# Another order table for the two local-attention layers of a one-core Trainium2 kernel

## The chip, the core and the metric

The kernel runs on one core of one Trainium2 chip. The core has a matmul engine (TensorE, PE in the profile, with its weight loads as PEld), a vector engine (DVE), an activation engine (ScalarE, ACT), a general engine (GpSimd, POOL) and a queue engine that only starts transfers (SyncE, SP). Each engine works through its own list of instructions in order and waits on semaphores where it needs another engine's result. The metric is the device time in microseconds (us), as the median of several executions; lower is better.

## The reference, cut to what matters

Input is `x` of shape (4, 1024, 256) in float32. It is normalised, and the output is `x` plus a gated attention of 16 heads over a window of 64 plus the output of two layers. This is one layer; the change concerns the two layers alone:

```python
def _layer(x, wqkv, qs, ksc, wo, lg, lb, w1, b1, w2, b2):
    h = shift_token(x)                        # half of the columns from the token before
    q, k, v = split(h @ wqkv)                 # 8 heads of 64
    q, k = rotary_xpos(l2norm(q) * qs, l2norm(k) * ksc)
    o = local_attention(q, k, v)              # softmax over a window of 128 keys back
    x = x + o @ wo
    h = layernorm(shift_token(x)) * lg + lb
    a, g = split(h @ w1 + b1)                 # hidden width 682
    return x + (a * gelu(g)) @ w2 + b2
```

## The kernel before, in words

There are two phases. `attention_phase` does the normalisation and the gated attention in the first 650 us; `layers_phase` does the two layers. The layers phase goes over 8 sequences (4 of the batch, for two layers; `it` 0 to 7) and over two halves of 512 tokens each. So the same pass over a half runs 16 times, from 702 us to the end at 1961 us, about 79 us each. I call such a pass a half.

What each engine does in a half is not worked out at run time. The list `ORDER` names 109 steps, and every engine walks the same list and emits its own share of each step. So the place of a step in the list sets where its instructions stand in the list of each engine that has a share of it. Steps that no common engine takes part in may change places freely. Within a half, the attention and feed-forward of this half are done, and at the same time the queries, keys and values of the next half are prepared.

The steps that the prediction speaks of, with what each engine does in them (number n is one of 8 units of two heads and two token tiles, or one of 4 tiles):

- `scores n`: PE, 24 small matmuls (L1497) into one of two pairs of score banks, which waits until `softmax n-2` has read them; DVE, mask and row maximum (L1713, four pieces).
- `softmax n`: ACT, four exponentials (L1639). `weigh n`: DVE, one reciprocal (L1721); POOL, four multiplications (L1380).
- `transpose n`: PE, into two banks (L1508 and L1512); ACT, copies (L1587, L1590, L1591). `values n`: PE (L1530) into `o_bank`; `take_o n` then empties it: ACT (L1645), DVE (L1724).
- `transpose_x`: PE, 8 transposes of the next half's rows (L1423) into two banks; ACT copies the high part (L1599), DVE the low part (L1672).
- `project_qk n`: PE, two products of 12/2 matmuls (L1416); ACT, copy and square of each (L1611, L1617); DVE, sums of squares and a clamp (L1677, L1681); POOL, the power -0.5 (L1362).
- `rope n`: DVE (L1688, L1689), POOL (L1368). `rope_sum n`: DVE (L1696, L1699). `transpose_qk n`: PE (L1469), ACT copies (L1593).
- `up n`: PE, 12 matmuls (L1555), or 6 where n is 5 or 11; ACT gelu (L1655), DVE product (L1775), ACT high part (L1659), DVE low part (L1779). `down n`: PE, 6 matmuls, or 4 where n is 5 or 11 (L1570).
- `load_wqkv`: ACT starts three transfers of 1 MB of weights (L88), once in the run, in the first half of `it` 3, since the layer changes after that sequence. `load_x`: SP starts the load of the rows that a later `transpose_x` reads.

PE writes all transposes and products in turn into three banks; a fill waits until the bank's last content, three fills back, has been taken:

```python
def take_bank(it, n):
    fill = filled.upto(it, n) - 1
    if fill >= 3:
        pe.wait_ge(*vacated(fill - 3))
    return bank_of(it, n)
```

`project_qk` counts as taken when DVE has summed its squares, `transpose` and `transpose_qk` when ACT has copied them, `transpose_x` when DVE has taken the low part.

## Time and profile before

| | us |
|---|---|
| median of 3 runs | 1965.38 |
| lowest and highest run | 1961.76, 1968.51 |
| the profiled execution, its own time | 1963.38 |
| its span, first to last instruction | 1961.3 |
| its mean granted TensorE clock | 0.982 |
| PE busy | 1836.3 (94%) |
| ACT, DVE, POOL busy | 1377.8, 1244.0, 903.6 |
| a half, between the ends of two | 78.6 to 80.3 |

All views below are of this one execution. Times at the start of a row are us from the start of the span. A row of the timeline has start, duration, engine, line, operation with its tiles, and how many instructions it merges; in brackets stands how long the engine was idle before it and who ended that. The half shown most is the one from 938.5 us, the second half of the second sequence.

### The profile page before, as it was taken

What the parts mean: (1) busy time and instruction counts of PE and PEld (TensorE: products, weight loads), DVE (VectorE), ACT (ScalarE), POOL (GpSimd) and SP (SyncE); (2) the same over time, 40 slices, a digit from 0 to 9 for tenths busy, and PEclk for the clock granted to TensorE, in tenths of its full rate; (3) what the DMA queues carried; (4) which work ended last, traced back from release to release, by engine and by line L of the source; (5) the groups of instructions that cost most, each with busy time, mean ns of one, the idle gap of its engine ahead of it and who ended that gap; (6) DMA issues with size and microseconds to landing.
All of it is one profiled execution on the core that took longest, in us unless ns stands there. A gap on an engine that the chain in (4) does not pass through costs nothing.

```text
span 1961.3 us, 47714 instructions
## 1 busy us (share of the span) xinstructions
PE 1836.3 (94%) x17808; PEld 1565.5 (80%) x17808; DVE 1244.0 (63%) x4126; ACT 1377.8 (70%) x3998; POOL 903.6 (46%) x1302
## 2 busy tenths in 40 slices
PE   6999999999999789999999999999999999999998
PEld 4788788788778568788788887887888878888787
DVE  4544543454443467777777777777777776777765
ACT  5886987878688465766857757668577585675854
POOL 3533543434344553735626437255364562654621
PEclk9999999999999889999999999999999999999989
DMA  4321320422324511110110101305112112010110
GB/s 146 100 76 55 116 87 34 116 76 77 87 75 150 180 47 28 39 53 23 47 45 23 54 17 50 122 15 168 37 39 63 34 47 66 18 60 25 42 47 28
DMA packets 125018, 128.11 MB, mean 65 GB/s; under 512 B 26632, under 2 KB 100082, under 8 KB 124788
## 3 DMA queue, kind: packets, MB, share of 16 engines
q1 hardware_dynamic: 121620, 118.77, 19.5%
q10 hardware_dynamic: 3168, 6.29, 0.9%
q8 instruction: 142, 2.33, 0.5%
q14 instruction: 88, 0.72, 0.1%
HBM read 72.44 MB, written 36.85 MB: 56 GB/s over the span
## 4 chain that ended last, share of the span: by engine, by line
PE 58%; ACT 11%; DVE 11%; POOL 11%; issue 5%; DMA 2%; SPq 1%; DVEq 0%; POOLq 0%; ACTq 0%
PE a_bank L630 15%; PE f_bank L1555 10%; PE f_bank L1416 9%; PE f_scores L1570 5%; POOL f_prob L1380 5%; PE a_o_bank L727 4%; ACT f_prob L1639 3%; PE f_o_bank L1530 3%; PE f_scores L1497 3%; PE a_bank L712 2%; PE a_scores L704 2%; POOL f_qk_tok L1368 2%; DVE f_scores L1713 2%; POOL f_norm L1362 1%; POOL a_prob L610 1%
## 5 line engine op out<-in xcount | busy, mean ns | idle before, releaser
L610 POOL TENSOR_SCALAR a_prob<-a_prob,a_row_inv,a_gate 128x128 f32<-128x128 f32 x512 | 226.3, 459 | 379.9 <-DVE a_row_inv L948 379.9
L1380 POOL TENSOR_SCALAR f_prob<-f_prob,f_row_inv 128x192 f32<-128x192 f32 x512 | 244.6, 495 | 319.6 <-DVE f_row_inv L1721 319.6
L1416 PE MATMUL f_bank<-weights,f_actT 128*128 128x512 f32 x1152 | 300.7, 406 | 1.5 <-DVE f_actT L1672 1.5
L1555 PE MATMUL f_bank<-f_hT,f_w 128*128 128x256 f32 x2112 | 269.1, 283 | 1.0 <-DVE f_gu L1775 1.0
L1555 PEld LDWEIGHTS f_bank<-f_hT,f_w 128*128 128x128 f32 x2112 | 258.4, 188 | 4.0 <-DVE f_gu L1775 2.7
L1416 PEld LDWEIGHTS f_bank<-weights,f_actT 128*128 128x128 f32 x1152 | 209.6, 191 | 48.2 <-ACT f_probT L1587 3.1
L1368 POOL TENSOR_TENSOR f_qk_tok<-f_qk_tok,tables 128x512 f32<-128x512 f32 x128 | 164.8, 1308 | 149.3 <-DVE f_sin_part L1689 149.3
L1639 ACT ACTIVATE f_prob<-f_scores,f_neg_max 128x192 f32<-128x192 f32 x512 | 207.9, 426 | 17.2 <-DVE f_neg_max L1713 15.9
L1713 DVE CUSTOM_DVE_ANT_0 f_scores<-f_scores,f_mask 128x192 f32<-128x192 f32 x512 | 166.3, 387 | 69.3 <-PE f_scores L1497 69.2
L1362 POOL TENSOR_TENSOR f_norm<-f_norm,f_minus_half 128x16 f32<-128x16 f32 x64 | 189.3, 2959 | 34.4 <-DVE f_norm L1681 31.5
L630 PE MATMUL a_bank<-a_xT,weights 128*128 128x512 f32 x768 | 195.6, 405 | 1.5 <-DVE a_wgate L917 1.5
L838 ACT ACTIVATE a_prob<-a_scores,a_neg_max 128x128 f32<-128x128 f32 x512 | 179.4, 391 | 24.1 <-DVE a_neg_max L939 24.0
L1659 ACT ACTIVATE f_u<-f_gu 128x256 fp32r<-128x256 f32 x192 | 80.2, 418 | 152.2 <-DVE f_gu L1775 152.2
L630 PEld LDWEIGHTS a_bank<-a_xT,weights 128*128 128x128 f32 x768 | 143.1, 191 | 36.8 <-issue 3.1
L1779 DVE TENSOR_TENSOR f_u<-f_gu,f_u 128x256 fp32r<-128x256 f32 x192 | 98.4, 513 | 93.0 <-ACT f_u L1659 93.0
L1570 PE MATMUL f_scores<-f_w,f_u 128*128 128x256 f32 (+1 forms) x1088 | 150.5, 283 | 0.0
L1497 PE MATMUL f_scores<-f_kT,f_q 64*64 64x128 f32 (+2 forms) x3072 | 117.9, 286 | 32.4 <-ACT f_prob L1639 31.7
L939 DVE CUSTOM_DVE_ANT_0 a_scores<-a_scores,a_mask 128x128 f32<-128x128 f32 x512 | 129.9, 324 | 26.0 <-PE a_scores L704 25.8
L1497 PEld LDWEIGHTS f_scores<-f_kT,f_q 64*64 64x64 f32 x3072 | 98.6, 137 | 56.9 <-ACT f_prob L1639 35.1
L1570 PEld LDWEIGHTS f_scores<-f_w,f_u 128*128 128x128 f32 (+1 forms) x1088 | 138.4, 189 | 2.9 <-DVE f_u L1779 1.5
L1655 ACT ACTIVATE f_gu<-f_bank,f_rows 128x256 f32<-128x256 f32 x192 | 89.6, 467 | 69.2 <-PE f_bank L1555 67.8
L952 DVE TENSOR_TENSOR a_o<-a_o_bank,a_o 128x512 fp32r<-128x512 f32 x64 | 44.1, 689 | 119.8 <-ACT a_o L845 119.8
(143 smaller groups left out, 4021.6 us busy)
## 6 DMA issues: line engine op xcount, KB each, us to landing
split_weights<-a_hi_lo SPq DMA_DIRECT2D x16, 512.0 KB, 3.0
x_next<-states SPq DMA_DIRECT2D x32, 256.0 KB, 3.2
tables<-scaled_tables SPq DMA_DIRECT2D x16, 512.0 KB, 6.0
f_x<-states SPq DMA_DIRECT2D x16, 512.0 KB, 5.3
split_weights<-a_hi_lo SPq DMA_DIRECT2D x12, 682.0 KB, 4.6
weights<-split_weights ACTq DMA_DIRECT2D x6, 1024.0 KB, 9.3
f_w<-split_weights SPq DMA_DIRECT2D x4, 1280.0 KB, 11.7
f_v_crossed<-f_v SPq DMA_DIRECT2D x40, 128.0 KB, 2.4
```

The costliest lines, as they stand in the source:

```text
L610: last = nc.gpsimd.tensor_scalar(part, part, row_inv[:, a % 2, head, t:t + 1], gate[:, half, t, h:h + 1], ALU.mult, ALU.mult)
L630: last = nc.tensor.matmul(out, lhs(c, a), rhs(c, b), start=(i == 0), stop=(i == len(order) - 1))
L838: e = nc.scalar.activation(prob[:, a % 2, head, t, :], scores[a % 2][head][:, t, :], ACT.Exp, bias=neg_max[:, a % 2, head, t:t + 1], scale ...
L1362: nc.gpsimd.tensor_tensor(n, n, minus_half[:], ALU.pow).then_inc(norm_ready.sem, 1)
L1368: last = nc.gpsimd.tensor_tensor(by_head(qk_tok[:, a % TILES])[:, which], by_head(qk_tok[:, a % TILES])[:, which], table(COS, a % TILES)[: ...
L1380: last = nc.gpsimd.tensor_scalar(part, part, row_inv[:, a % 2, head, t:t + 1], 1.0, ALU.mult, ALU.mult)
L1416: last = nc.tensor.matmul(out, lhs(c, a), rhs(c, b), start=(i == 0), stop=(i == len(order) - 1))
L1497: mm = nc.tensor.matmul(scores[a % 2][head][queries, t, place:place + keys.stop - keys.start], q[rows, pair, col:col + P][:, queries], kT[ ...
L1555: mm = nc.tensor.matmul(out[:, which * PART:(which + 1) * PART], w1[:, wp, c, col:col + P], hT[:, hp, c, columns_of(a // FH)], start=(i == ...
L1570: mm = nc.tensor.matmul(y_banks[a // FH % PARTS][:, t, :], u[0:k, a % GATED, up, t * P:(t + 1) * P], w2[0:k, wp, j, :], start=(j == 0 and ...
L1639: last = nc.scalar.activation(prob[:, a % 2, head, t, :], scores[a % 2][head][:, t, 0:KEYS], ACT.Exp, bias=neg_max[:, a % 2, head, t:t + 1 ...
L1713: last = nc.vector.tensor_tensor_reduce(out=sc, in0=sc, in1=mask[:, t + 1 if half or tile or t else 0], scale=-1.0, scalar=3e38, op0=ALU.a ...
```

## The change

Only the table `ORDER` is different: the same steps with the same numbers, in other places. Two of its lines, before and after:

```diff
-ORDER = [("softmax", 0), ("softmax", 1), ("scores", 0), ("scores", 1), ("weigh", 0), ("scores", 2), ("weigh", 1), ("transpose_x", 0),
+ORDER = [("softmax", 0), ("scores", 0), ("scores", 1), ("weigh", 0), ("weigh", 1), ("softmax", 1), ("transpose_x", 0), ("scores", 2),
```

Seen by engine, few places differ in a half. PE: `transpose_x` goes ahead of `scores 2`; `values 2` goes behind `transpose 3` and `project_qk 2`; `down 5` ahead of `up 9`; `transpose_qk 2` ahead of `down 6`; `down 9` ahead of `transpose_qk 3`. ACT: `softmax 3` ahead of `take_o 0`; `take_o 1` ahead of `transpose_qk 0`; `load_wqkv` from behind `transpose_h 1` to the end of the half. DVE: `scores 2` goes behind `weigh 1` and `transpose_x`; `ln_stats 1` goes ahead of `up 2`. POOL: nothing. SP: `load_x` from the first place to behind `shift_back`.

The first place is the start of a half on PE. Before, the 8 transposes of `x_next` (`transpose_x`) stand behind the matmuls of `scores 2` (the last three rows of L1497 ahead of them), and `transpose 0` follows:

```order
L1497 MATMUL f_scores<-f_kT,f_q 64x192 x2
L1497 MATMUL f_scores<-f_kT,f_q 64x128 x2
L1497 MATMUL f_scores<-f_kT,f_q 64x64 x2
L1423 MATMUL f_bank<-ident,x_next 128x128 x8
L1508 MATMUL f_bank<-ident,f_prob 128x128 x4
L1512 MATMUL f_bank<-ident,f_prob 128x128 x2
```

Now the same place reads as follows; the rows of L1497 behind `x_next` are `scores 2`, the one ahead of it is the end of `scores 1`:

```order
L1497 MATMUL f_scores<-f_kT,f_q 64x64 x2
L1423 MATMUL f_bank<-ident,x_next 128x128 x8
L1497 MATMUL f_scores<-f_kT,f_q 64x192 x2
L1497 MATMUL f_scores<-f_kT,f_q 64x128 x2
L1497 MATMUL f_scores<-f_kT,f_q 64x64 x2
L1497 MATMUL f_scores<-f_kT,f_q 64x192 x2
L1497 MATMUL f_scores<-f_kT,f_q 64x128 x2
L1497 MATMUL f_scores<-f_kT,f_q 64x64 x2
L1508 MATMUL f_bank<-ident,f_prob 128x128 x4
```

So the 8 transposes moved from behind a step that waits for `softmax 0` to ahead of it.

The second place is the middle of the attention on PE, around `project_qk 2` (the 12 matmuls of L1416). Before, `values 2` (L1530) comes first, then `transpose 3` (L1508, L1512) and `project_qk 2`:

```order
L1530 MATMUL f_o_bank<-f_probT,f_v 64x256 x2
L1530 MATMUL f_o_bank<-f_probT,f_v 64x64 x2
L1530 MATMUL f_o_bank<-f_probT,f_v_crossed 64x64 x2
L1508 MATMUL f_bank<-ident,f_prob 128x128 x4
L1512 MATMUL f_bank<-ident,f_prob 128x128 x2
L1416 MATMUL f_bank<-weights,f_actT 128x512 x12
```

Now:

```order
L1508 MATMUL f_bank<-ident,f_prob 128x128 x4
L1512 MATMUL f_bank<-ident,f_prob 128x128 x2
L1416 MATMUL f_bank<-weights,f_actT 128x512 x12
L1530 MATMUL f_o_bank<-f_probT,f_v 64x256 x2
L1530 MATMUL f_o_bank<-f_probT,f_v 64x64 x2
L1530 MATMUL f_o_bank<-f_probT,f_v_crossed 64x64 x2
```

`values 2` moved behind both, so PE asks for the banks of `transpose 3` and `project_qk 2` earlier by the length of `values 2`.

The third place is on ACT in the one half in which the weights of the next layer are loaded. Before, the three transfers stand behind the copy of `transpose_h 1` (L1599), amid the gelus:

```order
L1599 ACTIVATE f_hT<-f_bank 128x2x256
L88 DMA weights<-split_weights 128x4x512 x3
L1655 ACTIVATE f_gu<-f_bank,f_rows 128x256
L1659 ACTIVATE f_u<-f_gu 128x256
L1655 ACTIVATE f_gu<-f_bank,f_rows 43x256
```

Now they stand behind the copies of `transpose_qk 3` (L1593), ahead of the next half's first exponentials:

```order
L1593 ACTIVATE f_q<-f_bank 128x4x128
L1593 ACTIVATE f_kT<-f_bank 128x4x128
L88 DMA weights<-split_weights 128x4x512 x3
L1639 ACT_TABLE_LOAD
L1639 ACTIVATE f_prob,f_row_sum<-f_scores,f_neg_max 128x192 x8
```

They moved by seven gelus and to within ten us of their first reader.

## Rows read from the trace of the kernel before

**Rows 1.** The page, busy us (share of the span) of each engine.
```profile
PE 1836.3 (94%) x17808; PEld 1565.5 (80%) x17808; DVE 1244.0 (63%) x4126; ACT 1377.8 (70%) x3998; POOL 903.6 (46%) x1302
```

**Rows 2.** Windows, one half: length, busy us by engine, clock, DMA.
```profile
938.00:1017.00 79.00, 75.56 (x769) 66.54 (x768) 57.88 (x165) 53.92 (x151) 39.26 (x46) 0.98 0.12 36
```

**Rows 3.** Waits of PE from 700 us on: total us, times, longest.
```profile
PE f_scores L1497 <- ACT f_prob L1639: 31.7, 17, 2.1
PE f_bank L1508 <- POOL f_prob L1380: 16.6, 31, 1.2
```

**Rows 4.** Timeline of PE, start of the half.
```profile
938.45 1.75 PE L1497 MATMUL f_scores<-f_kT,f_q 64*64 64x192 f32 x48
942.15 0.89 PE L1497 MATMUL f_scores<-f_kT,f_q 64*64 64x192 f32 x24 [1.95 <-ACT f_prob L1639]
942.97 1.92 PE L1423 MATMUL f_bank<-ident,x_next 128*128 128x128 f32 x8
944.68 1.06 PE L1508 MATMUL f_bank<-ident,f_prob 128*128 128x128 f32 x4
```

**Rows 5.** Timeline of POOL, ACT and DVE in the same stretch.
```profile
942.51 1.62 POOL L1380 TENSOR_SCALAR f_prob<-f_prob,f_row_inv 128x192 f32<-128x192 f32 x4 [16.08 <-DVE f_row_inv L1721]
...
945.55 0.69 DVE L1672 TENSOR_TENSOR f_actT<-f_bank,f_actT 128x512 fp32r<-128x512 f32 x1 [0.16 <-ACT f_actT L1599]
...
945.78 0.60 ACT L1587 ACTIVATE f_probT<-f_bank 128x512 f32<-128x512 f32 x1 [0.26 <-PE f_bank L1508]
...
947.05 0.42 ACT L1639 ACTIVATE f_prob<-f_scores,f_neg_max 128x192 f32<-128x192 f32 x1
```

**Rows 6.** Windows in the same stretch; the clock stands behind POOL's busy time.
```profile
944.00:945.00 1.00, 1.00 (x7) 1.00 (x6) 1.00 (x7) 0.67 (x2) 0.23 (x2) 0.50 0.00 0
```

**Rows 7.** Timeline of POOL through the attention.
```profile
953.20 2.91 POOL L1362 TENSOR_TENSOR f_norm<-f_norm,f_minus_half 128x16 f32<-128x16 f32 x1 [1.63 <-DVE f_norm L1681]
...
966.01 2.91 POOL L1362 TENSOR_TENSOR f_norm<-f_norm,f_minus_half 128x16 f32<-128x16 f32 x1
...
973.01 3.63 POOL L1380 TENSOR_SCALAR f_prob<-f_prob,f_row_inv 128x192 f32<-128x192 f32 x4
...
979.50 1.62 POOL L1380 TENSOR_SCALAR f_prob<-f_prob,f_row_inv 128x192 f32<-128x192 f32 x4
```

**Rows 8.** Timeline of PE at `transpose 7`, and of DVE in `rope_sum 1`.
```profile
978.58 1.03 PE L1469 MATMUL f_bank<-ident,f_qk_tok 128*128 128x128 f32 x8
980.47 0.41 PE L1508 MATMUL f_bank<-ident,f_prob 128*128 128x128 f32 x2 [0.85 <-ACT f_kT L1593]
981.18 0.44 PE L1508 MATMUL f_bank<-ident,f_prob 128*128 128x128 f32 x2 [0.30 <-POOL f_prob L1380]
...
973.75 1.23 DVE L1696 TENSOR_TENSOR f_qk_tok<-f_qk_tok,f_sin_part 128x1024 f32<-128x1024 f32 x1
```

**Rows 9.** Timeline around `project_qk 2`.
```profile
957.79 1.50 DVE L1677 TENSOR_REDUCE f_norm<-f_square 128x8 f32<-128x512 f32 x2
...
958.20 0.77 PE L1530 MATMUL f_o_bank<-f_probT,f_v 128*64 128x256 f32 x8
...
959.25 0.66 PE L1508 MATMUL f_bank<-ident,f_prob 128*128 128x128 f32 x4
...
959.88 3.05 PE L1416 MATMUL f_bank<-weights,f_actT 128*128 128x512 f32 x12
```

**Rows 10.** Timeline of the end of this half.
```profile
1015.53 2.14 PE L1570 MATMUL f_scores<-f_w,f_u 128*128 128x256 f32 x16
...
1016.44 0.42 DVE L1779 TENSOR_TENSOR f_u<-f_gu,f_u 42x256 fp32r<-42x256 f32 x1 [0.48 <-ACT f_u L1659]
```

**Rows 11.** The weight transfers at 1237 us; then PE's first product behind them.
```profile
L88 ACTq DMA_DIRECT2D weights<-split_weights x3: 386/583/596, 1237.2 to 1238.3; - x3
...
DMA to landing us min/median/max: 6.1/8.4/10.5
...
1264.29 3.04 PE L1416 MATMUL f_bank<-weights,f_actT 128*128 128x512 f32 x12
```

More of the change, by code:

```diff
@@ new lines @@
+ORDER = [("softmax", 0), ("scores", 0), ("scores", 1), ("weigh", 0), ("weigh", 1), ("softmax", 1), ("transpose_x", 0), ("scores", 2),
+         ("transpose", 0), ("softmax", 2), ("transpose", 1), ("scores", 3), ("weigh", 2), ("project_qk", 0), ("softmax", 3), ("values", 0),
+         ("take_o", 0), ("load_x1", 0), ("weigh", 3), ("rope", 0), ("values", 1), ("scores", 4), ("transpose", 2), ("project_qk", 1),
+         ("softmax", 4), ("scores", 5), ("transpose", 3), ("weigh", 4), ("rope_sum", 0), ("project_qk", 2), ("values", 2), ("scores", 6),
+         ("softmax", 5), ("weigh", 5), ("rope", 1), ("take_o", 1), ("values", 3), ("transpose_qk", 0), ("transpose", 4), ("scores", 7),
+         ("softmax", 6), ("weigh", 6), ("project_qk", 3), ("project_o", 0), ("transpose", 5), ("softmax", 7), ("values", 4), ("values", 5),
+         ("rope_sum", 1), ("load_tables", 0), ("load_others", 0), ("weigh", 7), ("take_o", 2), ("ln_stats", 0), ("transpose", 6),
+         ("project_v", 0), ("transpose_qk", 1), ("transpose", 7), ("ln_apply", 0), ("take_o", 3), ("rope", 2), ("values", 6), ("values", 7),
+         ("project_v", 2), ("transpose_h", 0), ("project_o", 1), ("rope_sum", 2), ("shift_keys", 0), ("shift_front", 0), ("up", 0),
+         ("up", 1), ("ln_stats", 1), ("up", 2), ("project_v", 1), ("down", 0), ("down", 1), ("project_v", 3), ("ln_apply", 1), ("up", 3),
+         ("down", 2), ("transpose_h", 1), ("rope", 3), ("up", 4), ("down", 3), ("up", 5), ("up", 6), ("up", 7), ("down", 4),
+         ("shift_back", 0), ("up", 8), ("down", 5), ("up", 9), ("rope_sum", 3), ("load_x", 0), ("cross_values", 0), ("transpose_qk", 2),
+         ("down", 6), ("up", 10), ("up", 11), ("down", 7), ("down", 8), ("down", 9), ("transpose_qk", 3), ("add_attended", 0), ("out", 0),
+         ("out", 1), ("load_wqkv", 0), ("down", 10), ("down", 11)]
```

13 lines of the change are left out of this document (removed).

## The prediction

> **What bounds the kernel now.** I read the page first: PE is busy 94% of the span, and ACT, DVE and POOL far less [rows 1]. That share is an average over two phases, and the table is only used in the second, so I asked for windows of one half each. In the half from 938 us PE is busy 75.56 of 79 us [rows 2]. The other 3.4 us are what an order can win; the work itself is the same before and after. Then I read whom PE waits for. Two waits make nearly all of it: `scores 2` waits for the exponentials of `softmax 0`, 31.7 us in 17 waits, so about 2 us in each half; and the transposes of the weighed probabilities wait for POOL, 16.6 us in 31 waits [rows 3].
>
> The timeline shows where these lie. At the start of a half PE issues `scores 0` and `scores 1`, is done at 940.2 us (938.45 + 1.75) and stands idle until 942.15, when ACT has let go of the first score banks [rows 4]. In the stretch that follows, ACT and DVE hand things to each other: the copy of `transpose 0` starts at 945.78 and `softmax 2` at 947.05, behind the copies [rows 5].
>
> The second bound is POOL. It starts the first power of `project_qk 0` at 953.20, after an idle 1.63 us that DVE ended, and from there it has no idle until `weigh 7` ends at 981.12 (979.50 + 1.62) [rows 7]. PE arrives at `transpose 7` at about 979.6 (978.58 + 1.03) and can go on only at 980.47 and 981.18, after the first and the second half of `weigh 7` [rows 8]. The first of these waits is put down to ACT, but POOL's first two pieces end at 980.3 (979.50 + 0.82), so it is POOL. Behind 981.6 PE runs without a gap to the end of the half. So a half is: start (softmax and copies), then POOL's run of 28 us, then PE's 36 us. A gain at the start counts if it moves the start of POOL's run; PE alone has 0.9 to 1.5 us to spare ahead of `transpose 7`.
>
> **The change, part by part.**
>
> Start of the half. `transpose_x` goes into the idle 1.95 us. Its banks are free and its rows are loaded half a pass earlier. Eight transposes take 1.92 us at the low clock [rows 4, 6]; four others take 0.66 at the full one [rows 9], so 8 take between 1.3 and 1.9 us and fit into 940.2 to 942.15. `scores 2` stays where it is, since ACT sets it. `transpose 0` then stands at 943.0 and no longer at 944.68, but its first head comes from POOL at 943.33 (942.51 + 0.82) and its second at 944.13 [rows 4, 5]. I take the end of its first part at 944.55 against 945.74 before. ACT copies the two x banks from 943.6 and 944.1, so ends at 944.7 and not 945.5, and DVE's low parts end 0.6 earlier than 946.24 (945.55 + 0.69). DVE now does `scores 2` only behind them, from 945.6, and its first head is there at 946.4. ACT is through with `transpose 0` at about 946.4 too, so `softmax 2` starts at 946.45 against 947.05 [rows 5]. Gain 0.6 us. From above it is bounded by the whole idle of 1.95 us, from below by 0: if DVE's late `scores 2` takes it back, `softmax 2` stays at 947.0.
>
> Clock. PE idles from 940.2 to 942.15, and the granted clock then falls to 0.50 (1.2 GHz) for about three us, while the x transposes and `transpose 0` run [rows 6]. With 0.8 us of idle ahead of `scores 2` in place of 1.95 the fall may stay away. That helps the 0.6 to come true and I add nothing for it.
>
> POOL's run. `project_qk 0` follows `softmax 2` and the copies of `transpose 1` on ACT, so it moves by the same 0.6, and so does POOL's start. `softmax 3` ahead of `take_o 0` fills an idle moment in which ACT waits for the values; ACT is not what POOL waits for, so I count 0. Inside the run POOL waits at one place nearly for DVE: the power of `project_qk 2` at 966.01 [rows 7].
>
> Middle. `values 2` (1.05 us, from 958.20 to 959.25 [rows 9]) no longer separates `scores 5` from `transpose 3` and `project_qk 2`. `project_qk 2` needs the bank of `project_qk 1`, which DVE frees at 959.29 (957.79 + 1.50) before and 0.4 earlier after, at 958.9. PE would be ready at 958.2, so it waits 0.7 us there, a new stall, and starts at 959.0 in place of 959.88 [rows 9]. `values 2` now follows, so `scores 6` comes at 959.0 + 3.0 + 1.05 = 963.0, against 962.9 before. This eats PE's own gain and leaves it at `transpose 7` as late as before, 979.6; POOL ends there at 980.5 in place of 981.12. Cost 0 as long as PE's slack of 0.9 us covers it. DVE's part of `project_qk 2` even comes earlier, so POOL's power at 966.01 moves along.
>
> A collision on POOL. `weigh 6` takes 3.63 us at 973.01 while `weigh 7` takes 1.62; beside the long one runs DVE's `rope_sum 1` from 973.75 [rows 7, 8]. `rope_sum 1` hangs on PE's `project_o 0`, which I leave where it is, and `weigh 6` starts 0.6 earlier. Then three of its four pieces (0.41 each) are done before DVE starts. That could win up to 2.0 us of POOL's run, of which PE can use 0.9 beyond the 0.6. The other bound is a loss of as much in another place, since `weigh 3` and `weigh 4` would meet other DVE work. I take +0.15 us, near zero, since the two ends are equally far and only the one collision is seen in the row.
>
> The Trainium skill (SBUF — State Buffer, § SBUF: two separate sides) says that POOL and DVE share one port pair as an exclusive lock, also against DVE operations with two SBUF inputs, and that the later one blocks for the whole instruction. `rope_sum` has two SBUF inputs, and 3.63 against 1.62 us agrees. By that rule alone, a `weigh 6` that is ahead would lose nothing and the collision term would be its upper end; the sum would be that of the third rival, 13.5.
>
> End of the half. `down 5` (4 matmuls, at 2.14 / 16 us each [rows 10] 0.5 us) now precedes `up 9`. So the gelu of `up 9`, `rope_sum 3` and the chain of `up 10` and `up 11` on DVE come up to 0.5 later. The last low part ends at 1016.86 (1016.44 + 0.42), and PE needs it for the last four matmuls of the run of 16 that ends at 1017.67, so at 1017.1 [rows 10]: 0.25 us of cover. Loss between 0 and 0.3 us; I take 0.1, since most halves have a DVE that is a little ahead of the one shown. `transpose_qk 2` and `down 9` only change places among PE work, and ACT's copies of `transpose_qk 3` wait for ACT itself: 0. `ln_stats 1` ahead of `up 2` delays that one's low part by 1.4 us, hidden behind the values products on PE: 0. `load_x` is early enough in both: 0.
>
> Once in the run, `load_wqkv` comes right ahead of the half that begins near 1255. Its three issues take ACT about 0.58 us each [rows 11], 1.7 us, and a part of this lies in ACT's wait for the first row maxima (`scores 0` must run and be masked first): I take 0.9. The transfers land 6.1 to 10.5 us after their issue, so at 1261 to 1265 if issued from 1254.5 on, beside the loads of the new half; `project_qk 0` needs the first at 1264.3 and the second 1.5 us later [rows 11]. Loss 0 to 2 more; I take 0.6. Together 1.5.
>
> **Sum**, against the profiled execution of 1963.38 us: 15 halves (the last has no next half to prepare; I leave it at 0) times 0.6 + 0.15 - 0.1 = 0.65 gives 9.8, less 1.5 makes 8.3 us. The median of the runs shown is 1965.38, 2.0 above the profiled one; the forecast for the median is 1965.4 - 8.3 = 1957 us.
>
> **Rivals.**
> - Nothing arrives. DVE is behind two more waits at the start (the reciprocal of `weigh 1`, then the low parts) before `scores 2`, and the 0.6 dies there; what remains is the end of the half and the load: 15 x 0 + 1.5, with the small terms 1964 to 1967, say 1965. For it: the margin between DVE and ACT at `softmax 2` is 0.05 us. Against it: both get their inputs from the x banks 0.6 earlier.
> - Slower. The place is the end of the half: DVE's chain of `up 10` and `up 11` slips by the whole 0.5 us, PE waits for it ahead of `down 11`, and the next half starts late. It decides from the point where the slip exceeds 0.25 us and the start gives nothing. 16 x 0.5 + 1.5 = 9.5: 1975 us. Against it: `rope_sum 3` stands between and can take up some of it.
> - Much faster. POOL's run loses the collision; PE can use 0.6 + 0.5 us per half with its slack: 15 x 1.0 - 1.5 = 13.5, and with the clock not falling up to 20: 1946 to 1952, say 1950.
>
> **Chances.** Forecast 0.45, nothing 0.25, much faster 0.17, slower 0.13. A difference under 0.3% (5.9 us) can't be told from none with this kernel. The forecast's own range, 1953 to 1962, lies with 0.8 of it beyond that bound: faster 0.36 + 0.17 and a little, 0.54; same 0.09 + 0.23, 0.32; slower 0.14. The range for 8 in 10 is 1944 to 1969; the forecast's own is named above.
>
> **What would show it.** PE's wait of 1.95 us ahead of L1497 falls to 0.8; L1423 runs in 1.2 us and not 1.9; `softmax 2` starts 8.0 us after `scores 0` in place of 8.6 (947.05 - 938.45); POOL's run starts 0.6 earlier in the half and stays without idle; a new wait of L1416 on DVE's L1677 of about 0.7 us appears; the half is 0.65 us shorter. I am wrong in the mechanism if POOL's run starts no earlier, or if PE waits longer at the end of a half.

## The result, and the profile after

The changed kernel takes 1936.47 us (median of 4 runs, 1933.33 to 1939.64) against 1964.41 us for the kernel before in the same series. The ratio is 0.9856, with a 95% interval of 0.9832 to 0.988. It is 28 us faster, where I had forecast 8, and the time lies below my range. The profiled execution's span went from 1961.3 to 1934.0 us. The direction was right and the size was not. The experiments show that four fifths of the gain are lost without one step that I had counted at 0. Two slow executions, of 4267 us (the kernel before) and of 6876 us (the changed kernel without `softmax 3`), are left out of all ratios.

The page first. PE is as busy as before in us; POOL has lost 21.4 us of busy time and DVE 13.1, though all of them do the same instructions [rows 1]:

```profile
PE 1833.6 (95%) x17808; PEld 1564.8 (81%) x17808; DVE 1230.9 (64%) x4126; ACT 1377.1 (71%) x3998; POOL 882.2 (46%) x1302
```

I read the difference as waiting inside the instructions, since the instructions are the same; the rows below bear it out for POOL and DVE. The chain that ended last says where this mattered. Before, by engine:

```profile
PE 58%; ACT 11%; DVE 11%; POOL 11%; issue 5%; DMA 2%; SPq 1%; DVEq 0%; POOLq 0%; ACTq 0%
```

After:

```profile
PE 76%; ACT 11%; DVE 5%; POOL 3%; DMA 2%; issue 2%; SPq 1%; DVEq 0%; POOLq 0%; ACTq 0%
```

The waits of PE from 700 us on, after (line waited for: us in total, times, longest), answer to [rows 3]:

```profile
PE f_scores L1497 <- ACT f_prob L1639: 15.1, 15, 2.0
PE f_bank L1508 <- POOL f_prob L1380: 12.9, 34, 1.1
...
PE f_bank L1416 <- DVE f_norm L1677: 4.0, 15, 0.3
```

The first wait fell by 16.6 us in all. The half that answers to the one of [rows 4 to 8] starts at 932.44. In the timeline of PE `transpose_x` (L1423) fills a part of the wait and runs at the full clock; `project_qk 2` (L1416) has the new wait on DVE, 0.27 us; and `transpose 7` (L1508 behind L1469) has no wait any more, where it had 0.85 and 0.30 [rows 8]:

```profile
932.44 1.74 PE L1497 MATMUL f_scores<-f_kT,f_q 64*64 64x192 f32 x48
934.11 1.09 PE L1423 MATMUL f_bank<-ident,x_next 128*128 128x128 f32 x8
936.13 0.89 PE L1497 MATMUL f_scores<-f_kT,f_q 64*64 64x192 f32 x24 [0.93 <-ACT f_prob L1639]
...
952.49 3.06 PE L1416 MATMUL f_bank<-weights,f_actT 128*128 128x512 f32 x12 [0.27 <-DVE f_norm L1677]
...
971.81 1.03 PE L1469 MATMUL f_bank<-ident,f_qk_tok 128*128 128x128 f32 x8
972.68 0.70 PE L1508 MATMUL f_bank<-ident,f_prob 128*128 128x128 f32 x4
```

On POOL in the same half `weigh 6` takes 1.62 us in place of 3.63, and the power of `project_qk 3` behind it (L1362) takes 3.88 us and not 2.90 (from 976.61 in the trace of before), so one of the two us is given back:

```profile
946.38 2.91 POOL L1362 TENSOR_TENSOR f_norm<-f_norm,f_minus_half 128x16 f32<-128x16 f32 x1 [1.63 <-DVE f_norm L1681]
...
965.82 1.62 POOL L1380 TENSOR_SCALAR f_prob<-f_prob,f_row_inv 128x192 f32<-128x192 f32 x4
967.41 3.88 POOL L1362 TENSOR_TENSOR f_norm<-f_norm,f_minus_half 128x16 f32<-128x16 f32 x1
971.27 1.62 POOL L1380 TENSOR_SCALAR f_prob<-f_prob,f_row_inv 128x192 f32<-128x192 f32 x4
```

I number the halves 0 to 15 and measure each from its first row of L1713 to the next half's (the half of the rows ahead is No. 3), and half 15 up to its last additions to `x` (L1785). Worked out this way, halves 0 to 14 have a mean length of 79.25 us before and 77.61 after, which is 15 x 1.64 = 24.6 us, and half 15 went from 65.42 to 62.67. `weigh 6` took 3.26 us on average before and takes 1.63 after.

### The profile page after: what moved, and what is told of

The parts are those of the page before. It is cut to its first block, busy times and chain, and to the rows that moved or that the text cites. A ratio compares the mean times of both kernels' runs of the same rounds, so it can differ in the third digit from the quotient of the medians.

```text
span 1934.0 us, 47714 instructions
## 1 busy us (share of the span) xinstructions
PE 1833.6 (95%) x17808; PEld 1564.8 (81%) x17808; DVE 1230.9 (64%) x4126; ACT 1377.1 (71%) x3998; POOL 882.2 (46%) x1302
## 4 chain that ended last, share of the span: by engine, by line
PE 76%; ACT 11%; DVE 5%; POOL 3%; DMA 2%; issue 2%; SPq 1%; DVEq 0%; POOLq 0%; ACTq 0%
PE f_bank L1416 18%; PE a_bank L630 16%; PE f_bank L1555 12%; PE f_scores L1570 6%; PE f_o_bank L1530 5%; PE a_o_bank L727 4%; PE f_scores L1497 3%; ACT f_prob L1639 3%; PE a_bank L712 2%; PE a_scores L704 2%; PE f_bank L1469 2%; PE f_bank L1508 2%; POOL a_prob L610 2%; ACT a_prob L838 1%; PE f_bank L1512 1%
## 5 line engine op out<-in xcount | busy, mean ns | idle before, releaser
L1380 POOL TENSOR_SCALAR f_prob<-f_prob,f_row_inv 128x192 f32<-128x192 f32 x512 | 212.6, 434 | 310.7 <-DVE f_row_inv L1721 310.7
L1416 PE MATMUL f_bank<-weights,f_actT 128*128 128x512 f32 x1152 | 305.0, 411 | 5.6 <-DVE f_norm L1677 4.0
L1416 PEld LDWEIGHTS f_bank<-weights,f_actT 128*128 128x128 f32 x1152 | 213.2, 194 | 56.2 <-DVE f_norm L1677 7.8
L1639 ACT ACTIVATE f_prob<-f_scores,f_neg_max 128x192 f32<-128x192 f32 x512 | 208.0, 427 | 14.4 <-DVE f_neg_max L1713 13.1
L1362 POOL TENSOR_TENSOR f_norm<-f_norm,f_minus_half 128x16 f32<-128x16 f32 x64 | 200.4, 3131 | 36.7 <-DVE f_norm L1681 35.0
L1659 ACT ACTIVATE f_u<-f_gu 128x256 fp32r<-128x256 f32 x192 | 80.3, 418 | 177.6 <-DVE f_gu L1775 177.6
L1713 DVE CUSTOM_DVE_ANT_0 f_scores<-f_scores,f_mask 128x192 f32<-128x192 f32 x512 | 166.4, 388 | 32.6 <-PE f_scores L1497 32.6
L1570 PE MATMUL f_scores<-f_w,f_u 128*128 128x256 f32 (+1 forms) x1088 | 155.3, 285 | 0.6 <-DVE f_u L1779 0.3
L1497 PE MATMUL f_scores<-f_kT,f_q 64*64 64x128 f32 (+2 forms) x3072 | 118.8, 288 | 15.9 <-ACT f_prob L1639 15.1
L1497 PEld LDWEIGHTS f_scores<-f_kT,f_q 64*64 64x64 f32 x3072 | 99.6, 138 | 37.9 <-ACT f_prob L1639 18.9
L1677 DVE TENSOR_REDUCE f_norm<-f_square 128x8 f32<-128x512 f32 x128 | 86.1, 683 | 59.8 <-ACT f_square L1617 59.5
```

Of the source, the lines that this page charges most:

```text
L1362: nc.gpsimd.tensor_tensor(n, n, minus_half[:], ALU.pow).then_inc(norm_ready.sem, 1)
L1380: last = nc.gpsimd.tensor_scalar(part, part, row_inv[:, a % 2, head, t:t + 1], 1.0, ALU.mult, ALU.mult)
L1416: last = nc.tensor.matmul(out, lhs(c, a), rhs(c, b), start=(i == 0), stop=(i == len(order) - 1))
L1497: mm = nc.tensor.matmul(scores[a % 2][head][queries, t, place:place + keys.stop - keys.start], q[rows, pair, col:col + P][:, queries], kT[ ...
L1570: mm = nc.tensor.matmul(y_banks[a // FH % PARTS][:, t, :], u[0:k, a % GATED, up, t * P:(t + 1) * P], w2[0:k, wp, j, :], start=(j == 0 and ...
L1639: last = nc.scalar.activation(prob[:, a % 2, head, t, :], scores[a % 2][head][:, t, 0:KEYS], ACT.Exp, bias=neg_max[:, a % 2, head, t:t + 1 ...
```

## A pair of halves in the trace of before that tells it

The reason can be seen without any new run. Halves 12 and 14 of the kernel before are the same program, both at the even place. The power of `project_qk 0` starts 13.58 us into the one (1669.04 - 1655.46) and 13.59 into the other. Yet half 12 takes 79.47 us (1655.46 to 1734.93) and half 14 takes 77.60 (1815.01 to 1892.61). The table ahead of the prediction gives 78.6 to 80.3 us for a half; over halves 0 to 14 it is 77.60 to 80.59, and half 14 is the one that this range hid. Half 12 in the timeline of DVE, then POOL:

```profile
1655.46 0.36 DVE L1713 CUSTOM_DVE_ANT_0 f_scores<-f_scores,f_mask 128x192 f32<-128x192 f32 x1 [0.36 <-PE f_scores L1497]
...
1674.70 1.38 DVE L1681 TENSOR_SCALAR f_norm<-f_norm 128x16 f32<-128x16 f32 x1
...
1734.93 0.36 DVE L1713 CUSTOM_DVE_ANT_0 f_scores<-f_scores,f_mask 128x192 f32<-128x192 f32 x1 [0.36 <-PE f_scores L1497]
...
1669.04 2.91 POOL L1362 TENSOR_TENSOR f_norm<-f_norm,f_minus_half 128x16 f32<-128x16 f32 x1 [1.63 <-DVE f_norm L1681]
1671.94 1.62 POOL L1380 TENSOR_SCALAR f_prob<-f_prob,f_row_inv 128x192 f32<-128x192 f32 x4
1673.53 2.52 POOL L1368 TENSOR_TENSOR f_qk_tok<-f_qk_tok,tables 128x512 f32<-128x512 f32 x2
...
1679.06 2.26 POOL L1380 TENSOR_SCALAR f_prob<-f_prob,f_row_inv 128x192 f32<-128x192 f32 x4
...
1688.44 3.55 POOL L1380 TENSOR_SCALAR f_prob<-f_prob,f_row_inv 128x192 f32<-128x192 f32 x4
```

Half 14:

```profile
1815.01 0.37 DVE L1713 CUSTOM_DVE_ANT_0 f_scores<-f_scores,f_mask 128x192 f32<-128x192 f32 x1 [0.36 <-PE f_scores L1497]
...
1834.26 0.17 DVE L1681 TENSOR_SCALAR f_norm<-f_norm 128x16 f32<-128x16 f32 x1
...
1892.61 0.37 DVE L1713 CUSTOM_DVE_ANT_0 f_scores<-f_scores,f_mask 128x192 f32<-128x192 f32 x1 [0.36 <-PE f_scores L1497]
...
1833.08 2.52 POOL L1368 TENSOR_TENSOR f_qk_tok<-f_qk_tok,tables 128x512 f32<-128x512 f32 x2
...
1838.47 1.62 POOL L1380 TENSOR_SCALAR f_prob<-f_prob,f_row_inv 128x192 f32<-128x192 f32 x4
...
1847.07 1.64 POOL L1380 TENSOR_SCALAR f_prob<-f_prob,f_row_inv 128x192 f32<-128x192 f32 x4
1848.67 3.98 POOL L1362 TENSOR_TENSOR f_norm<-f_norm,f_minus_half 128x16 f32<-128x16 f32 x1
```

The first thing that differs is L1681, the clamp of `project_qk 1`, an instruction on 128x16 numbers. In half 12 it is recorded as starting at 1674.70, as POOL's second piece of `rope 0` begins (two pieces in 2.52 us from 1673.53), and it takes 1.38 us, until that piece is over. In half 14 it gets through in 0.17. From there on the rows differ as follows. DVE has lost 1.2 us, so its `rope_sum 0` runs beside `weigh 4` (2.26 us, not 1.62). POOL's `weigh 6` starts 0.92 us later in the half, while `rope_sum 1` starts at the same place, and so the two meet (3.55 us, not 1.64). The power behind it gives a us back (2.90 against 3.98). The whole costs 1.87 us of the half. The clamp is caught in halves 1 to 13 of the kernel before and free in halves 0 and 14 alone. What decides is small: by the records the clamp starts 0.061 us ahead of POOL's second piece in half 12 and 0.066 us ahead in half 14.

Half 14 is not shorter for being the last but one. In the kernel with all but the start changed (below) the clamp is free in both, and they take 77.55 and 77.56 us; with `values 2` alone moved it is caught in half 14, which takes 79.47.

The Trainium skill (SBUF — State Buffer, § SBUF: two separate sides) says of the port pair that POOL shares with DVE instructions in a 2-port mode or with two SBUF inputs: the one that starts first has it for its whole instruction and the other blocks. The trace agrees in that the clamp is held until POOL's piece is over. It does not agree in the order, since the clamp is recorded as starting first, by 0.06 us; and the clamp has one SBUF input, and no trace here shows its mode. I had cited this rule for `weigh 6` and not looked at which other rows it might bear on.

## The experiments

All ratios are to the kernel before, measured on the same chip in the same series, of 4 to 12 runs each; the interval is 95%. W6 is the length of `weigh 6` in the profiled execution, as the median over halves 2, 4 to 14 (even) and 1, 3 to 13 (odd). In two kernels the profiled execution was the slowest by far and does not stand for the ratio: start of the half alone (1959 us, the other five 1939 to 1949) and `softmax 3` alone (1953 us, the other five 1942 to 1945).

| edit | ratio | interval | W6 even, odd |
|---|---|---|---|
| before | 1 | | 3.55, 3.61 |
| changed kernel | 0.9856 | 0.9832 to 0.9880 | 1.63, 1.62 |
| start of the half alone | 0.9924 | 0.9895 to 0.9953 | 3.56, 3.60 |
| values 2 alone | 0.9987 | 0.9975 to 1.0000 | 3.55, 1.63 |
| start and values 2 | 0.9930 | 0.9910 to 0.9949 | 3.55, 2.67 |
| all but the start | 0.9899 | 0.9880 to 0.9918 | 1.65, 1.62 |
| start, values 2, softmax 3, take_o 1 | 0.9855 | 0.9838 to 0.9872 | 1.62, 1.62 |
| all but start and values 2 | 0.9883 | 0.9869 to 0.9898 | 1.66, 1.63 |
| all but take_o 1 | 0.9869 | 0.9850 to 0.9887 | 1.65, 1.64 |
| all but softmax 3 | 0.9970 | 0.9957 to 0.9983 | 3.56, 2.61 |
| softmax 3 alone | 0.9918 | 0.9897 to 0.9938 | 2.73, 2.61 |
| before, POOL 0.15 us more | 0.9917 | 0.9901 to 0.9933 | 2.71, 1.64 |
| start and softmax 3 | 0.9871 | 0.9850 to 0.9892 | 1.63, 2.62 |
| changed, transposes of x twice | 0.9816 | 0.9798 to 0.9834 | 1.63, 1.64 |
| start, transposes of x twice | 0.9938 | 0.9919 to 0.9958 | 3.56, 3.62 |
| changed, POOL 0.15 us more | 0.9877 | 0.9863 to 0.9892 | 1.66, 1.65 |
| changed, DVE two ops more | 0.9864 | 0.9848 to 0.9880 | 1.66, 1.65 |
| changed, DVE six ops more | 0.9926 | 0.9909 to 0.9943 | 3.56, 1.63 |
| start and softmax 3, transposes twice | 0.9848 | 0.9829 to 0.9867 | 1.63, 2.61 |

Where the expectations say "the first halves" they mean the odd numbers, and with "the second halves" the even ones.

### Which part of the table does it

Start of the half alone, on the kernel before:

```diff
-("weigh", 0), ("scores", 2), ("weigh", 1), ("transpose_x", 0),
+("weigh", 0), ("weigh", 1), ("transpose_x", 0), ("scores", 2),
```

> Only the start of the half is changed (PE: transpose_x ahead of scores 2; DVE: scores 2 behind weigh 1 and transpose_x). Theory A (two separate gains: the start gives about 0.65 us a half, values 2 gives the rest): softmax 2 comes at +6.7 us in the half in place of +7.4 on average, weigh 6 still takes over 3 us beside rope_sum 1, and PE is at transpose 7 no earlier than POOL allows; halves 0.6 to 0.8 us shorter, in all 10 to 12 us, ratio 0.994 to 0.995. Theory B (the start alone does it, since 0.6 us earlier is enough to put weigh 6 ahead of rope_sum 1): weigh 6 takes 1.6 us in most halves and the time is within 5 us of the changed kernel, ratio 0.986 to 0.989. Theory C (the start alone gives nothing because something later takes it back): ratio 0.998 to 1.000.

Measured 0.9924. By the profile it is Theory A's kind, though faster than it said: `softmax 2` at +6.68 us on average (7.36 before), `weigh 6` as long as ever. Its six runs spread from 1939 to 1959 us; in the profiled one, which was the slowest, six halves from No. 1 on have the low clock in their head and their power of `project_qk 0` at +13.9 us or later, where the others have it at +12.8. The profiled execution is only 2 us faster than the median of before on that chip, so it can't explain the 15 us of the median. The faster executions have a higher granted clock, up to 0.992 against 0.985; but two of 1948 and 1949 us have 0.985 as well. Whether the clamp was free in some of their halves is not shown.

`values 2` alone:

```diff
-("values", 2), ("transpose", 3), ("project_qk", 2),
+("transpose", 3), ("project_qk", 2), ("values", 2),
```

> Only values 2 is moved, behind transpose 3 and project_qk 2. Theory A: project_qk 2 starts up to 1 us earlier, its power on POOL too, weigh 6 is over before rope_sum 1 on DVE starts and takes 1.6 us in place of 3.3; norms 3 pays back some 0.7; the half is 0.6 to 1.0 us shorter, ratio 0.992 to 0.995. Theory B: PE waits 0.7 us for DVE's sums of project_qk 1, nothing comes earlier, weigh 6 stays at 3.3 us; ratio 0.999 to 1.001. In both the wait of 1.95 us at the start stays and the clock falls in the same halves as before.

Measured 0.9987. Neither theory is right: `weigh 6` does fall to 1.6 us in most odd halves, but the time is the same within its error.

Both together:

> Start of the half and values 2 changed together, the rest of the table as before. Theory A: about all of the change's gain, 1.3 to 1.6 us a half, ratio 0.986 to 0.989. If the rest (softmax 3, take_o 1, the end of the half, the two loads) carries a part of its own, this stays above 0.990.

Measured 0.9930. These two are half of the gain, and `values 2` adds nothing to the start alone. All but the start:

> The changed kernel with its start of the half put back (scores 2 ahead of transpose_x on PE, scores 2 ahead of weigh 1 on DVE). Theory A: the idle of 1.95 us ahead of scores 2 and the clock at 0.50 behind it are back; softmax 2 at +7.4 on average; weigh 6 stays short (1.6 us); 0.7 to 1.0 us a half lost against the changed kernel, ratio to before 0.992 to 0.995. Theory B (the start is what shortens weigh 6): weigh 6 is at 3.3 us again and the ratio is 0.998 to 1.001.

Measured 0.9899, below what Theory A said: without the start of the half 1% is left, more than I had forecast for the whole.

Four parts together, with the end of the half and the loads as before:

> Start of the half, values 2, softmax 3 ahead of take_o 0 and take_o 1 ahead of transpose_qk 0; the end of the half and the two loads as before. Theory F (the two steps on ACT carry the part that start and values 2 together do not give): weigh 6 is at 1.6 us in every half, as in the changed kernel, and the ratio is 0.985 to 0.988. Theory G (that part lies in the end of the half or in the loads): as start and values 2 together, weigh 6 at 3.55 in half of the halves, ratio 0.992 to 0.994.

Measured 0.9855, as the changed kernel. So the end of the half and the loads do nothing that these ratios can tell. Theory F holds. The complement, all but the start and `values 2`:

> Everything of the change except the start of the half and values 2. Theory F1 (softmax 3 alone moves POOL's run 0.4 us earlier, out of two collisions): weigh 3 falls from 2.05 to 1.67 us in the first halves, weigh 6 to rope_sum 1 stays at 0.7 us and collides still; ratio 0.997 to 0.999. Theory F2 (the steps on ACT are enough without values 2): weigh 6 at 1.6 us, ratio 0.990 to 0.993.

Measured 0.9883; Theory F2's mechanism, beyond its range. One step on ACT put back in each of the next two:

```diff
-("take_o", 1), ("values", 3), ("transpose_qk", 0),
+("values", 3), ("transpose_qk", 0), ("take_o", 1),
```

> The changed kernel with take_o 1 put back behind transpose_qk 0 on ACT. If take_o 1 matters (it frees the bank of the values for project work and DVE's share of it earlier), the halves get 0.5 us or more longer and weigh 6 is long again in some; ratio 0.989 to 0.992. If only softmax 3 matters, nothing changes: ratio 0.984 to 0.987.

Measured 0.9869: not told apart from the changed kernel.

```diff
-("softmax", 3), ("values", 0), ("take_o", 0),
+("values", 0), ("take_o", 0), ("softmax", 3),
```

> The changed kernel with softmax 3 put back behind take_o 0 on ACT. If softmax 3 matters: weigh 3 at 2.05 us again in the first halves, the power of project_qk 1 0.4 us later, weigh 6 at 2.7 to 3.6 us in many halves, ratio 0.990 to 0.993 as with start and values 2 alone. If not: ratio 0.984 to 0.987.

Measured 0.9970. Without `softmax 3` ahead of `take_o 0` four fifths of the gain are gone, 22 of 28 us. The clamp is caught in all 15 halves, for 1.31 to 1.37 us. The parts do not add up: this kernel has the start and `values 2`, which alone give 0.9930, and is slower than they are, with intervals that lie apart. In the profiles `rope_sum 1` starts 1.01 to 1.07 us behind `weigh 6` in its odd halves, and `weigh 6` takes 2.6 us in all of them; with the start and `values 2` alone it is 1.17 to 1.22 us, and `weigh 6` takes 1.62 in three of the seven. Then this step alone on the kernel before, and with the start:

> The kernel before with softmax 3 ahead of take_o 0 on ACT and nothing else. Theory P (DVE's tiny clamp of project_qk 1, L1681, is issued 0.01 to 0.07 us before POOL's second piece of rope 0 and is held for its whole length, 1.33 us in place of 0.17; DVE and POOL are late from there on, up to the collision of weigh 6 with rope_sum 1): softmax 3 brings DVE's rope 0 and this clamp forward by 0.1 to 0.4 us; clamp 0.2 us in the second halves, weigh 3 at 1.67 in the first ones, weigh 6 at 1.6 us everywhere, ratio 0.987 to 0.991, as in the kernel with everything but start and values 2 (0.988). Rival Q (it needs the end of the half, the load or take_o 1 too): ratio 0.994 to 1.000.

Measured 0.9918, between the two ranges. In the profiled execution, which is 10 us slower than the other five, the clamp is at 0.21 to 0.23 us in all even halves and `weigh 4` at 1.63, as said, but `weigh 6` stays at 2.6 to 2.7 in most halves. How it stands in the faster ones is not shown.

> The kernel before with the start of the half and softmax 3, without values 2, take_o 1, the end and the loads. If these two are the whole of the gain: ratio 0.984 to 0.987, the same as the changed kernel. If values 2 carries a part of its own once softmax 3 is moved: 0.988 to 0.990.

Measured 0.9871, a hair beyond the first range: these two are nearly the whole. What is missing shows in the odd halves, where `weigh 6` takes 2.62 us. In every kernel of the table with `softmax 3` moved, it is at 1.6 there if `values 2` or `take_o 1` is moved too, one of them being enough, and at 2.6 if neither is. The start of `weigh 6` is not what they change: in half 5 it is at +32.22 here and at +32.23 in the changed kernel. They make `rope_sum 1` later, which starts 1.11 us behind `weigh 6` here and 1.43 there. `weigh 6` is four pieces of 0.4 us, so with 1.43 us it is nearly over, with 1.11 the last piece is caught, and with the 0.74 of the kernel before one more (973.75 - 973.01) [rows 7, 8]. The distance does not decide alone: with `values 2` moved alone, `weigh 6` takes 1.6 us in five odd halves and 2.7 in two, at 1.18 to 1.22 us in all seven. Why the two moves make `rope_sum 1` later was not followed.

### Is it the clamp? Useless work as a test

If hundredths of a us decide on 1.9 us, then work that makes POOL a little later at the right place must make the kernel faster. The kernel before, with two memsets between the two pieces of `rope 0`:

```diff
                 for which in (QUERY, KEY):
+                    for j in range(2 * (which == KEY and a % TILES == 0)): pool.memset(pad[:, 8 * j:8 * j + 8], 0.0)
                     last = nc.gpsimd.tensor_tensor(...)
```

> The kernel before with 0.2 us of useless work more on POOL: two memsets of 128x8 between the two pieces of rope 0, once in a half. Its order is that of before. Theory P: the clamp of project_qk 1 on DVE now gets through ahead of POOL's second piece (0.17 to 0.25 us in place of 1.33), weigh 4 falls from 2.26 to 1.62 us and weigh 6 from 3.6 to 1.6 in the second halves at least; added work makes the kernel faster: 0.5 to 1.8 us a half, ratio 0.987 to 0.996. Rival Q (the clamp's length is only where DVE's waiting shows, and costs nothing): POOL's run is 0.2 us longer, ratio 1.001 to 1.003.

Measured 0.9917: 16 us faster by adding work. Its timeline in half 12 (lines behind 1367 are one higher in this kernel, so L1682 is the clamp and L1369 the rope):

```profile
1658.27 0.22 DVE L1682 TENSOR_SCALAR f_norm<-f_norm 128x16 f32<-128x16 f32 x1
...
1657.09 1.28 POOL L1369 TENSOR_TENSOR f_qk_tok<-f_qk_tok,tables 128x512 f32<-128x512 f32 x1
1658.31 0.15 POOL L1368 MEMSET f_pad<- 128x8 f32 x2
1658.41 1.29 POOL L1369 TENSOR_TENSOR f_qk_tok<-f_qk_tok,tables 128x512 f32<-128x512 f32 x1
...
1662.56 1.62 POOL L1381 TENSOR_SCALAR f_prob<-f_prob,f_row_inv 128x192 f32<-128x192 f32 x4
...
1671.17 2.71 POOL L1381 TENSOR_SCALAR f_prob<-f_prob,f_row_inv 128x192 f32<-128x192 f32 x4
```

The clamp is 0.14 us ahead of the second piece (1658.27 and 1658.41) and takes 0.22. That piece is only 0.09 us later in the half than before. The clamp is free in all 15 halves. What the theory said of `weigh 6` came out the other way round: 1.6 us in the odd halves and still 2.7 in the even ones, where `rope_sum 1` starts 1.3 us behind it. The same memsets in the changed kernel, as a control:

> The changed kernel with the same two useless memsets on POOL between the two pieces of rope 0 that made the kernel before 0.8% faster. Theory P (they help only where DVE's clamp of project_qk 1 would lose the race for the port): the clamp already gets through in the second halves, and in the first ones it comes 0.3 us into POOL's piece, which 0.1 to 0.2 us do not change: no difference, ratio to before 0.984 to 0.988. Rival (a pause on POOL helps everywhere): 0.976 to 0.982.

Measured 0.9877, no gain: where the clamp is free already, a pause does not help. In four even halves (0, 2, 8 and 12) `weigh 6` now takes 2.7 us. From the other side, the changed kernel with work added on DVE ahead of the clamp:

```diff
+                for j in range(2 * (a % TILES == 1 and it is not None)): nc.vector.reciprocal(pad[:, 16 * j:16 * j + 16], mask[:, 0, 0:16])
                 dve.wait_ge(emptied.sem, emptied.past(it, ("project_qk", a), KEY))
```

> The changed kernel with two reciprocals of 128x16 more on DVE (0.3 us together, into a place nobody reads) just ahead of the clamp of project_qk 1. Theory P: in the second halves the clamp, which came 0.14 us ahead of POOL's second piece of rope 0, now comes behind its start and takes 1.0 to 1.3 us in place of 0.2; weigh 4 at 2.26 again; POOL's run 0.9 us later there; 0.6 to 0.9 us in 7 or 8 halves, 5 to 8 us in all, ratio to before 0.988 to 0.991. Rival (DVE has idle time and 0.3 us are hidden, as its 64% of busy time says): ratio 0.984 to 0.987.

Measured 0.9864: the rival's number. The two instructions moved the clamp by 0.15 us, to the very start of POOL's piece in the even halves, and it still got through, in 0.11 us. So I made it six of 128x4:

> As the kernel with two reciprocals more on DVE ahead of the clamp of project_qk 1, but six of 128x4, since with two the clamp was recorded at the very start of POOL's second piece in the second halves and still got through (0.11 us). Six take about 0.6 us, so the clamp comes 0.2 to 0.4 us into that piece. Theory P: it is then held until the piece ends, about 0.9 to 1.1 us; weigh 4 at 2.26 in the second halves too, POOL's run 0.8 us later there, the second halves as long as the first (77.0 to 77.7 in place of 76.2 to 76.8 where the clock is full): 5 to 7 us in all, ratio to before 0.988 to 0.991. Rival (DVE's slack hides it): 0.984 to 0.987.

Measured 0.9926. Half 12 of this kernel (L1682 is the clamp, L1680 the added work):

```profile
1660.68 0.48 DVE L1680 RECIPROCAL f_pad<-f_mask 128x4 f32<-128x4 f32 x6
1661.09 1.19 DVE L1682 TENSOR_SCALAR f_norm<-f_norm 128x16 f32<-128x16 f32 x1
...
1659.72 2.52 POOL L1368 TENSOR_TENSOR f_qk_tok<-f_qk_tok,tables 128x512 f32<-128x512 f32 x2
...
1665.25 2.27 POOL L1380 TENSOR_SCALAR f_prob<-f_prob,f_row_inv 128x192 f32<-128x192 f32 x4
...
1674.63 3.56 POOL L1380 TENSOR_SCALAR f_prob<-f_prob,f_row_inv 128x192 f32<-128x192 f32 x4
```

Half a us of work on an engine that is busy 64% of the time brings all three back in the even halves, the caught clamp, the long `weigh 4` and the long `weigh 6`, while the odd ones, where DVE got the same work, keep their `weigh 6` of 1.63 us. So it is not the added work by itself that costs. Its half 12 takes 78.74 us, and 76.83 with the two reciprocals. Theory P holds in kind; I had priced it at 0.6 to 0.9 us for each even half, without the collision of `weigh 6`, which makes it 1.9.

### The clock

The changed kernel with `transpose_x` done twice into the same place:

```diff
-                    for t in range(TILES):
+                    for t in (*range(TILES), *range(TILES)):
```

> The changed kernel with every transpose of transpose_x done twice into the same place, 8 transposes of useless PE work more in a half (0.66 to 1.3 us), which lie in the wait of 0.93 us for softmax 0. Theory R (the granted clock falls to 0.50 in the head of some halves since PE idles there, and costs up to 2.5 us in a half): with the wait filled no stretch of the layers has a low clock, halves 10, 12 and 14 are 77 to 78 us in place of 79.3; ratio 0.978 to 0.983. Rival S (the clock falls for another reason, or the copies of the x banks come too late for softmax 2): as the changed kernel or worse, 0.985 to 0.990.

Measured 0.9816, 1924.75 us, the best kernel of all (the changed one is at 0.9856). The windows of half 10 in the changed kernel, with PE's granted clock behind the busy times:

```profile
1474.60:1479.40 4.80, 3.13 (x60) 2.44 (x52) 3.03 (x19) 4.10 (x19) 1.86 (x5) 1.00 0.60 204
1479.50:1486.30 6.80, 6.46 (x41) 4.96 (x40) 3.72 (x19) 4.37 (x15) 2.07 (x7) 0.50 0.19 75
...
```

The same half in the kernel with the doubled transposes:

```profile
1472.10:1476.90 4.80, 4.00 (x68) 3.31 (x60) 3.01 (x19) 4.09 (x19) 1.85 (x5) 1.00 0.61 201
1477.00:1483.80 6.80, 6.29 (x62) 4.58 (x62) 4.43 (x20) 6.44 (x19) 2.91 (x8) 1.00 0.20 78
...
```

PE is busy 4.00 of the first 4.80 us in place of 3.13, and the clock stays at its upper level (2.4 GHz) where it had gone to the lower one (1.2 GHz) for 6.8 us. The timeline of PE, the changed kernel:

```profile
1475.15 1.09 PE L1423 MATMUL f_bank<-ident,x_next 128*128 128x128 f32 x8
1477.17 0.89 PE L1497 MATMUL f_scores<-f_kT,f_q 64*64 64x192 f32 x24 [0.93 <-ACT f_prob L1639]
...
1483.55 4.32 PE L1416 MATMUL f_bank<-weights,f_actT 128*128 128x512 f32 x12
```

And with the transposes twice:

```profile
1472.67 1.97 PE L1423 MATMUL f_bank<-ident,x_next 128*128 128x128 f32 x16
1474.69 0.89 PE L1497 MATMUL f_scores<-f_kT,f_q 64*64 64x192 f32 x24
...
1479.74 3.06 PE L1416 MATMUL f_bank<-weights,f_actT 128*128 128x512 f32 x12
```

The wait of 0.93 us is filled, `scores 2` stands where it stood, and `project_qk 0` takes 3.06 us and not 4.32. Half 10 goes from 79.33 to 76.74 us. No half from No. 1 to No. 14 has a low clock any more, and the mean length of halves 0 to 14 falls from 77.61 to 76.99 us, 9 us in all. Theory R holds, with 0.9816 at the slow end of what it said. The intervals of the two ratios just touch, so the gain rests on the profiles as much as on them. Twice on two less complete kernels:

> The kernel before with the start of the half changed and each transpose of transpose_x done twice; softmax 3 and all else as before. Weigh 6 stays at 3.6 us by either theory. Theory R (the clock is a part of its own, beside the collisions): no low clock in the layers, softmax 2 at +6.6 us, power of project_qk 0 at +12.8 us in every half; every half as the undisturbed ones of the kernel with the start alone (78.1 to 78.7 us), so 10 to 13 us less than before and no spread between its runs: ratio 0.987 to 0.991, below the 0.9924 of the start alone. Rival S (the clock matters only where the collisions are gone): 0.992 to 0.995.

Measured 0.9938, the rival's number, and not below the 0.9924 of the start alone. In the profile the low clock is down from six of the halves 1 to 14 to two, but the clamp is caught in 13 of 15 halves. One of the six runs is at 1943 us and five are at 1953 to 1956, with granted clocks of 0.991 and 0.988 to 0.990, so more than the clock varies. Whether the clock is worth something while the collisions are there stays open.

> The kernel before with only the start of the half and softmax 3 changed, and the transposes of transpose_x done twice. Theory (the three mechanisms, start, clamp and clock, add up and the rest of the change is not needed): weigh 6 short, low clock nowhere or once in the layers, ratio 0.981 to 0.985 as for the changed kernel with the doubled transposes (0.9816). If values 2, the order of the end and the loads carry a part: 0.986 to 0.989.

Measured 0.9848, at the slow end of the first range. The whole change with the doubled transposes is at 0.9816, and the two intervals just touch, so the ratios leave open whether the rest carries a part. The clock is full in halves 1 to 14; the odd halves are 78.0 to 78.7 us long, against 77.1 to 78.0 in the kernel with all moves and the doubled transposes, and have the 2.6 us of `weigh 6`.

## Why the prediction was wrong

- **Start of the half, 0.6 us: right.** `softmax 2` starts 7.79 us after `scores 0` (8.0 said; 940.23 - 932.44), L1423 takes 1.09 us (1.2 said), PE's wait is 0.93 us (0.8 said), and over halves 0 to 14 `softmax 2` is 0.63 us earlier. Taken out of the changed kernel, the start costs 0.0043 of the ratio, 8.4 us, where I had said 15 x 0.6 = 9.
- **The clock, 0 added: wrong in size.** Halves 1 to 7 keep the full clock after the change, where three of them (2, 3 and 4) had a low stretch of 3.4 us before, but in halves 10, 12 and 14 it is at 0.50 for 6.8 us, and those take 79.3 us where 76.7 are possible. The change gains from the clock in one place and loses in the other, and the mean granted clock is 0.982 before and 0.983 after; filling the wait gives a further 0.4%.
- **"`softmax 3` ahead of `take_o 0` ... ACT is not what POOL waits for, so I count 0": this is the step that failed.** Taken out, the ratio is 0.9970 in place of 0.9856, so about 22 us hang on a step with a price of 0. POOL indeed never waits for ACT; but it waits for DVE, and DVE waits for ACT at this very place. In half 12 of the kernel before DVE stands still for 0.92 us until ACT has done `softmax 3`, ahead of the reciprocal of `weigh 3`. In the changed kernel (half 4) it waits for `take_o 0` instead, and the reciprocal follows at once:

```profile
1670.67 0.18 DVE L1721 RECIPROCAL f_row_inv<-f_row_sum 128x4 f32<-128x4 f32 x1 [0.92 <-ACT f_prob L1639]
...
1024.88 0.69 DVE L1724 TENSOR_TENSOR f_o<-f_o_bank,f_o 128x512 fp32r<-128x512 f32 x1 [1.20 <-ACT f_o L1645]
```

So the step moves DVE against POOL: DVE's `rope 0` (L1688) starts 1.72 us behind POOL's power in the even halves and 2.19 in the odd ones before, and 1.81 in both after. In the even halves the clamp starts 5.66 us behind the start of POOL's power before and 5.64 after; POOL's `weigh 3` ahead of the rope takes 1.67 us in place of 1.62. Together the clamp is then 0.12 to 0.15 us ahead of POOL's piece and not 0.06, and it is free. In the odd halves `weigh 3` takes 1.67 in place of 2.05; the clamp then starts 0.3 us into the piece and is held for 0.99 us, but POOL is 0.4 us earlier, and `weigh 6` is free if `values 2` or `take_o 1` has been moved too. The even half No. 4 of the changed kernel, DVE and POOL, against half 12 above:

```profile
1029.40 0.19 DVE L1681 TENSOR_SCALAR f_norm<-f_norm 128x16 f32<-128x16 f32 x1
...
1023.76 2.91 POOL L1362 TENSOR_TENSOR f_norm<-f_norm,f_minus_half 128x16 f32<-128x16 f32 x1 [1.62 <-DVE f_norm L1681]
1026.66 1.67 POOL L1380 TENSOR_SCALAR f_prob<-f_prob,f_row_inv 128x192 f32<-128x192 f32 x4
1028.29 2.53 POOL L1368 TENSOR_TENSOR f_qk_tok<-f_qk_tok,tables 128x512 f32<-128x512 f32 x2
...
1033.68 1.62 POOL L1380 TENSOR_SCALAR f_prob<-f_prob,f_row_inv 128x192 f32<-128x192 f32 x4
```

- **The collision term, +0.15 a half: mis-sized.** Its mechanism was right for `weigh 6`, and the upper end I wrote (2.0 us, of which PE can use 0.9) was the better number. The net of the freed clamp is 1.87 us in the pair of halves above. I also held `weigh 6` to depend on its own 0.6 us: moving the start alone leaves it at 3.6, since `rope_sum 1` moves along.
- **Middle, 0:** PE's new wait is 0.27 and not 0.7, and PE reaches `transpose 7` 0.9 us earlier in the half (40.24 us behind its start, 972.68 - 932.44, and 41.16 before). I had taken PE's slack to cap the gain; it did not, as the copies and sums in front came earlier too.
- **End of the half, -0.1, and the load, -1.5:** the load costs nothing that shows, since half 7, behind the moved load, takes 77.08 us and half 5 77.07. The end is not settled. The kernel with the old end and the old loads has the same ratio (0.9855), but 15 x 0.1 us is less than its interval can tell. In the profiles the halves with the full clock in both kernels (1, 2, 3, 6 and 7) are 0.03 to 0.11 us longer with the new end, and one 0.41, so a loss of 0.1 may be right.
- **Last half, 0:** 2.75 us. A part is the clock, which is low for 10.2 us of it before and for 6.8 after; in six of the kernels it is full there, and they take 61.6 to 61.8 us for this half, against 62.67. The rest stays open.

The third rival, at 0.17, was the nearest (1950), and it too was short. Its sum took 0.4 to 0.5 us a half for the freed collision, though the text on the collision had put PE's share at up to 0.9; the pair of halves shows 1.87. It named `weigh 6`; the clamp and the step on ACT, which free it in the even halves, stood in no rival.
